# A graph layer with gathered rows: how the edge lists, the statistics and the tables are set up

## The chip, the core and the metric

The kernel runs on one core of a Trainium2 chip. The metric is device time in microseconds (us) of one launch. The core has five engines with instruction streams of their own: PE (TensorE, matrix multiply), DVE (VectorE), ACT (ScalarE), POOL (GpSimd) and SP (SyncE, which here only issues DMA transfers). They meet only at semaphores. Transfers are issued from SP, ACT and POOL; SP's and ACT's go to a hardware queue each (q1 and q10 in the profile), POOL's gathers to a software queue (q0), and all of them share 16 DMA engines.

## The reference

There are N = 6250 nodes with 256 features and E = 100000 edges (src, dst, weight); dst is sorted.

```python
f = _layernorm(x)
h  = segment_sum(w[:, None] * (f @ W1)[src], dst) + b1          # convolution 1
x_ = leaky(concat([h, f[root]]))
x_ = segment_sum(w[:, None] * (x_ @ W2)[src], dst) + b2          # convolution 2
x_ = concat([leaky(x_), h[root]])
x  = x + leaky(x_ @ Wl + bl)
n  = _layernorm(x)
weights = n @ wr + br
sel = top_k(weights, N//2)[:-1]                                  # 3124 nodes
x  = x + n + scatter(sel, weights[sel] * (gelu(n[sel] @ fw1 + fb1) @ fw2 + fb2))
```

## The kernel before

**Nodes.** They are cut into 49 windows of 128 (NW). x lies in xs, one window per 256 columns. The normed rows are made in acc (f_rows is acc from slot A0 = 4 on) and are stored to f_dram, from which the first convolution gathers; the second one gathers from t2_dram ("conv_rows" in the profile). acc later holds the sums of the windows, so it is set to zero between the store and the first sums.

**Edges.** They are padded to 784 tiles of 128 edges (NT). Four tiles are a group, so there are 196 groups (NG); 16 tiles (RING) are a round, and the rounds run from the last to the first. Only 782 tiles hold an edge (781 full ones and 32 edges); the last two are padding with weight 0.

**The gather stream.** POOL issues one indirect DMA for each tile (L276 to L284): 128 rows of 1 KB into a slot of ring, eight groups deep. From the ninth group on it waits on group_used (L280), which DVE raises once the sums of an older group have been taken. For each tile PE multiplies the gathered rows with a 128x128 selection matrix S (L483 to L490) that DVE builds (L768), and DVE adds the group's sums to acc (L776). Where a group crosses into the next window there is a second set, S_more. The second convolution does the same from t2_dram, with the feed-forward part (L579 to L591) between the groups. At the end come a search for the router's threshold and the output.

**The start.** Before the first gather these things happen:
- SP loads x in five chunks XCH of ten windows (the last of nine, L232 to L236); window 48 has only 106 nodes and is a transfer of its own, behind xs_cleared.
- ACT issues the edge loads (L302 to L305): each list goes to a tile of 112 partitions with 7 pieces of 128 edges, as six pieces for all partitions, 109 rows of 128 edges for the seventh and one row for the rest. Then come the same dst values again as rows of 512 (dst_groups, L307 to L311), with 98, 97 and 1 rows.
- POOL turns the lists into floats (L265, L266). PE transposes them into PSUM (L462 to L466). DVE copies them out (L721 to L729) as idx (gather indices), dstc and wc.
- DVE computes the statistics of a chunk (normalise, L693 to L706: bn_stats, bn_aggr, an inverse square root by small steps). ACT applies them (L333 to L337). SP stores the chunk (L237 to L239).
- DVE takes the minimum and maximum of dst per group (L710 to L717), PE spreads them over the partitions (L468 to L473), and DVE makes the tables (L738 to L755).

DVE's order is: memsets, chunks 0 and 1, minimum and maximum, chunk 2, the copies of the turned edges and the root's index, chunks 3 and 4, tables, and, after the stores, memsets of acc (L854 to L857). ACT's order is: all edge loads, a table load for gelu, the five chunks, then the root's row, the weights, and a clear of part of acc (L350). POOL waits for edges_kept (L268) and for all stores (L272) before the first gather.

Of the kernel before, what the change touches and what calls it, by code (L numbers as in the profile page):

```python
# [17 lines left out]
def gnn_ffn_kernel(nc, x, src, dst, edge_weight, W1, b1, W2, b2, Wl, bl, root_idx,  # L18
# [5 lines left out]
    P = 128  # L24
    N, D = x.shape
# [19 lines left out]
    CH = 7  # L45
    CR = NT // CH
    SKEW = 4
# [14 lines left out]
    assert NT == CH * CR and NG == 2 * GR and CR <= P and GR <= P  # L62
# [6 lines left out]
    with ctx:  # L69
# [62 lines left out]
        nmax = sb("gmm", [P, 2, 2], i32)  # L132
# [19 lines left out]
        src_rows = rflat[0:CR, 0:EW].bitcast(i32).rearrange("p (c e) -> p c e", c=CH)  # L152
        dst_rows = rflat[0:CR, EW:2 * EW].bitcast(i32).rearrange("p (c e) -> p c e", c=CH)
        w_rows = rflat[0:CR, 2 * EW:3 * EW].rearrange("p (c e) -> p c e", c=CH)
        bst = rflat[:, 3 * EW:3 * EW + NW * 6].rearrange("p (w s) -> p w s", s=6)

        src_rowsf = rflat[0:CR, 0:EW].rearrange("p (c e) -> p c e", c=CH)
        dst_rowsf = rflat[0:CR, EW:2 * EW].rearrange("p (c e) -> p c e", c=CH)

        f_rows = acc[:, A0:A0 + NW, :]  # L160
        dst_groups = acc[0:GR, A0 + NW:A0 + NW + 2 * GE // D, :].rearrange("p r d -> p (r d)").bitcast(i32).rearrange("p (c e) -> p c e", c=2)
        diag = hT[:, :, :].rearrange("p c n -> p (c n)")[:, 0:4 * GR].rearrange("p (a c g) -> p a c g", a=2, c=2)
# [11 lines left out]
        edges_cleared, edges_loaded = sem("edges_cleared"), sem("edges_loaded")  # L174
        rows_floated, edges_turned, edges_kept = sem("rows_floated"), sem("edges_turned"), sem("edges_kept")
        groups_loaded = sem("groups_loaded")
# [4 lines left out]
        f_ready, f_stored = sem("f_ready"), sem("f_stored")  # L181
# [38 lines left out]
        ZCUT = NACC * 5 // 8  # L220
# [10 lines left out]
        def _(sp):  # L231
# [3 lines left out]
            sp.wait_ge(xs_cleared, 1)  # L235
            sp.dma_start(xs[0:LAST_ROWS, X0 + NW - 1, :], x[(NW - 1) * P:N, :]).then_inc(x_loaded[-1], 16)  # L236
            for c, (w0, w1) in enumerate(XCH):  # L237
                sp.wait_ge(f_ready, c + 1)
                sp.dma_start(f_dram[w0 * P:w1 * P, :].rearrange("(w p) d -> p w d", p=P), f_rows[:, w0:w1, :]).then_inc(f_stored, 16)  # L239
# [9 lines left out]
        def _(pool):  # L249
            link = Links(pool, pool_chain)  # L250

            nc.gpsimd.memset(src_rows[:, CH - 1, :], 0).then_inc(edges_cleared, 1)
            nc.gpsimd.memset(dst_rows[:, CH - 1, :], N - 1).then_inc(edges_cleared, 1)
            nc.gpsimd.memset(w_rows[:, CH - 1, :], 0.0).then_inc(edges_cleared, 1)
            nc.gpsimd.memset(dst_groups[:, 1, :], N - 1).then_inc(edges_cleared, 1)
# [4 lines left out]
            link(nc.gpsimd.memset(ident[:, :], 0.0))  # L260
            nc.gpsimd.affine_select(out=ident[:, :], in_=ident[:, :], compare_op=ALU.not_equal, fill=1.0, base=0,
                                    pattern=[[-1, P]], channel_multiplier=1).then_inc(consts_ready, 1)
# [4 lines left out]
            nc.gpsimd.iota(iota[:, :], pattern=[[1, 2 * P]], base=0, channel_multiplier=0).then_inc(iota_ready, 1)  # L267
# [26 lines left out]
        def _(act):  # L294
# [3 lines left out]
            full = (CH - 1) * CR * P  # L298
            part = (E - full) // P
            rest = E - full - part * P  # L300
            act.wait_ge(edges_cleared, 4)
            for a, r in ((src, src_rows), (dst, dst_rows), (edge_weight, w_rows)):  # L302
# [4 lines left out]
            gfull = E // GE - GR  # L307
            gend = (GR + gfull) * GE
            act.dma_start(dst_groups[:, 0, :], dst[0:GR * GE].rearrange("(r e) -> r e", e=GE)).then_inc(groups_loaded, 16)
            act.dma_start(dst_groups[0:gfull, 1, :], dst[GR * GE:gend].rearrange("(r e) -> r e", e=GE)).then_inc(groups_loaded, 16)  # L310
# [704 lines left out]
```

## Time and profile before

| | us |
|---|---|
| median of 3 runs | 2211.76 |
| lowest and highest run | 2207.11, 2212.53 |
| the profiled execution | 2209.72 |
| its span, first to last instruction | 2207.7 |
| mean granted TensorE clock | 0.915 of full speed |

Busy time in the span: PE 1693.9 us (77%), DVE 1149.4 (52%), ACT 371.0 (17%), POOL 1511.5 (68%). The mean DMA rate is 107 GB/s; in the first two fortieths of the span it is 193 and 183 GB/s. A row of the timeline reads: start, duration, engine, line, operation, output<-inputs, number of instructions merged, and in brackets the idle time of the engine ahead of it with what ended it. SPq and ACTq are the DMA issues of SP and ACT.

### The profile page before, as it was taken

How to read it: one execution, taken by the hardware profiler on the slowest of the kernel's cores; microseconds unless marked ns; L12 is line 12 of the kernel's file. 1: busy time of each engine (PE TensorE's matmuls, PEld its weight loads, DVE VectorE, ACT ScalarE, POOL GpSimd, SP SyncE). 2: the span in 40 equal slices, each digit the busy share in tenths (PEclk: the TensorE clock that was granted, in tenths of full speed). 3: DMA queues.
4: the chain of work that ended last, by engine and by line, in shares of the span. 5: the costliest groups of instructions: out<-in, count | busy, mean ns of one | idle time of the engine just before them, and what ended most of it. 6: DMA issues, size and time to landing. Idle time of an engine off the chain costs nothing.

```text
span 2207.7 us, 39619 instructions
## 1 busy us (share of the span) xinstructions
PE 1693.9 (77%) x7203; PEld 1361.6 (62%) x7204; DVE 1149.4 (52%) x4020; ACT 371.0 (17%) x938; POOL 1511.5 (68%) x1588
## 2 busy tenths in 40 slices
PE   0277777777767766767679999989998999988881
PEld 0165556555545554555468888878777777777660
DVE  5654445444444343333356666666565555555446
ACT  2300000000000000000112222222222222222230
POOL 1377777777777777777577777777777777777500
PEclk9998899888888888887899999999999999999995
DMA  6633333333333333333233333333333333333203
GB/s 193 183 111 109 110 111 109 109 112 111 108 112 112 111 109 110 112 110 109 81 106 104 103 104 102 103 104 105 104 103 104 105 104 103 103 104 105 76 0 116
DMA packets 109339, 236.70 MB, mean 107 GB/s; under 512 B 28862, under 2 KB 58683, under 8 KB 109310
## 3 DMA queue, kind: packets, MB, share of 16 engines
q0 software_dynamic: 75392, 205.62, 31.9%
q1 hardware_dynamic: 19048, 19.22, 2.7%
q10 hardware_dynamic: 14870, 11.58, 1.6%
q14 instruction: 24, 0.20, 0.0%
q8 instruction: 5, 0.08, 0.0%
HBM read 216.94 MB, written 19.38 MB: 107 GB/s over the span
## 4 chain that ended last, share of the span: by engine, by line
POOL 44%; PE 25%; issue 18%; DVE 5%; DMA 4%; DVEq 2%; ACTq 1%; ACT 0%; POOLq 0%
POOL ring L283 44%; PE ps_agg L489 13%; PE ps_dn L583 4%; PE ps_up L590 4%; DMA ring<-conv_rows,idx 2%; DMA ring<-normed_rows,idx 2%; DVE S L768 1%; ACTq L305 1%; DVE xs L990 1%; PE ps_dn L581 1%; PE ps_o L553 1%; PE ps_o L621 1%; DMA acc<-in_dst 1%; DVE acc L776 0%; DVE ring L699 0%
## 5 line engine op out<-in xcount | busy, mean ns | idle before, releaser
L489 PE MATMUL ps_agg<-ring,S 128*128 x3136 | 869.7, 426 | 342.7 <-DMA ring<-normed_rows,idx 162.1
L489 PEld LDWEIGHTS ps_agg<-ring,S 128*128 128x128 f32 x3136 | 643.7, 212 | 511.0 <-issue 416.6
L283 POOL DMA_INDIRECT ring<-normed_rows,idx x784 | 752.0, 959 | 282.8 <-issue 234.1
L283 POOL DMA_INDIRECT ring<-conv_rows,idx x784 | 752.9, 960 | 256.2 <-issue 231.6
L776 DVE TENSOR_TENSOR acc<-acc,ps_agg x490 | 206.5, 421 | 651.3 <-PE ps_agg L489 601.1
L768 DVE TENSOR_SCALAR S<-iota,dstc,wc 128x128 f32<-128x128 int16 x1584 | 448.5, 363 | 153.9 <-issue 124.2
L489 PE MATMUL ps_agg<-ring,S_more 128*128 x768 | 192.2, 395 | 19.8 <-DVE S_more L768 18.1
L583 PE MATMUL ps_dn<-fw2s,hT 128*128 128x256 f32 x864 | 206.2, 393 | 0.0
L590 PE MATMUL ps_up<-xnT,fw1s 128*128 128x256 f32 x832 | 190.5, 382 | 1.2 <-ACT hT L400 1.2
L583 PEld LDWEIGHTS ps_dn<-fw2s,hT 128*128 128x128 f32 x864 | 163.4, 194 | 39.6 <-issue 18.6
L489 PEld LDWEIGHTS ps_agg<-ring,S_more 128*128 128x128 f32 x768 | 150.5, 199 | 54.0 <-issue 32.1
L590 PEld LDWEIGHTS ps_up<-xnT,fw1s 128*128 128x128 f32 x832 | 154.1, 190 | 20.4 <-ACT hT L400 1.6
L364 ACT ACTIVATE stage<-acc 128x256 f32 x103 | 42.9, 417 | 441.5 <-DVEq L802 432.6
L768 DVE TENSOR_SCALAR S_more<-iota,dmore,wc 128x128 f32<-128x128 int16 x384 | 111.0, 365 | 8.9
L400 ACT ACTIVATE hT<-ps_up,fb1c 128x256 f32<-128x256 f32 x212 | 83.0, 478 | 59.7 <-PE ps_up L590 59.7
L374 ACT ACTIVATE xnT<-ps_t 128x256 f32<-128x256 f32 x50 | 19.2, 384 | 436.2 <-PE ps_t L542 426.5
L758 DVE SCALAR_TENSOR_TENSOR zT<-yT 128x256 f32<-128x256 f32 x103 | 44.0, 427 | 40.7 <-DVE acc L776 32.2
L553 PE MATMUL ps_o<-W2s,zT 128*128 128x256 f32 x200 | 59.7, 423 | 0.0
L389 ACT ACTIVATE yT<-ps_h,b1c 128x128 f32<-128x128 f32 x100 | 31.3, 364 | 156.9 <-PE ps_h L562 156.9
L562 PEld LDWEIGHTS ps_h<-xnT,W1s 128*128 128x128 f32 x400 | 55.0, 199 | 3.1
L434 ACT ACTIVATE xn<-rows,norm 128x256 f32<-128x256 f32 x53 | 31.9, 603 | 137.3 <-DVE norm L921 137.3
L562 PE MATMUL ps_h<-xnT,W1s 128*128 128x128 f32 x400 | 54.8, 282 | 0.0
(175 smaller groups left out, 981.9 us busy)
## 6 DMA issues: line engine op xcount, KB each, us to landing
ring<-normed_rows,idx POOLq DMA_INDIRECT x784
ring<-conv_rows,idx POOLq DMA_INDIRECT x784
conv_rows<-rows ACTq DMA_DIRECT2D x50, 128.0 KB
out_rows<-xs SPq DMA_DIRECT2D x6, 896.0 KB
xs<-in_x SPq DMA_DIRECT2D x4, 1280.0 KB, 14.3
normed_rows<-acc SPq DMA_DIRECT2D x4, 1280.0 KB, 5.2
normed_rows<-acc SPq DMA_DIRECT2D x1, 1152.0 KB, 4.8
xs<-in_x SPq DMA_DIRECT2D x1, 1024.0 KB
```

The lines of the kernel that those rows point to most:

```text
L283: pool.indirect_dma_start(out=ring[:, slot * TG + t, :], out_offset=None, in_=f_dram if l == 0 else t2_dram, in_offset=bass.IndirectOffset ...
L364: nc.scalar.activation(stage[:, :], flat(acc[:, ds(within(act.snap(s * -1 + (NW - 1 + A0)), NACC - 1), 1), :]), ACT.Copy).then_inc(staged[ ...
L400: last = nc.scalar.activation(hT[:, b * HB + c, :], ps_up[:, c, :], ACT.Gelu_apprx_tanh, bias=fb1c[:, b * HB + c:b * HB + c + 1])
L434: nc.scalar.activation(xn[:, :], rows[:, :], ACT.Identity, scale=rinv1, bias=nmr1).then_inc(xn_ready, 1)
L489: last = nc.tensor.matmul(to, select[:, t, :], moving, start=(t == 0), stop=(t == TG - 1))
L553: last = nc.tensor.matmul(ps_o[:, 0:D], zT[:, k, :], W2s[:, k, :], start=False, stop=(k == KC - 1))
L562: last = nc.tensor.matmul(ps_h[:, c * P:(c + 1) * P], W1s[:, k, c * P:(c + 1) * P], aggT[:, k, :], start=(k == 0), stop=(k == KC - 1))
L583: last = nc.tensor.matmul(ps_dn[:, 0:D], hT[:, c, window * P:(window + 1) * P], fw2s[:, c, :], start=False, stop=(c == HC - 1))
L590: last = nc.tensor.matmul(ps_up[:, c, :], fw1s[:, k, (b * HB + c) * P:(b * HB + c + 1) * P], xnT[:, k, :], start=(k == 0), stop=(k == KC - 1))
L758: return V.scalar_tensor_tensor(to, of, SLOPE, of, ALU.mult, ALU.max)
L768: last = V.tensor_scalar(to[:, t, :], iota[:, 0:P], at, wc[:, ds(column, 1)], ALU.is_equal, ALU.mult)
L776: V.tensor_tensor(to, to, flat(ps_agg[:, ds((i + 1) & 1, 1), 0:D]), op=ALU.add).then_inc(acc_step[l], 1)
```

## The change

- **Edge lists** are loaded as 98 rows of 1024 edges, 4 KB contiguous per partition: 96 rows in one transfer, one row, and the rest of the last row (672 edges). CH is 8 and CR is 98. The padding is set by three small DVE memsets ahead of all other DVE work, in place of four POOL memsets. The separate dst_groups load is gone: minimum and maximum are taken from the turned-to-float dst rows, two groups a row.
- **Each list has its own semaphore**. POOL clamps src while it turns it to float, then turns dst; PE transposes a list when it is there; **ACT copies** the turned lists out of PSUM (six activations, written with a stride of 8 columns) ahead of its chunk work.
- **DVE** computes the statistics of all five chunks first, then minimum and maximum, the root's index, and the tables.
- **XCH runs from the last node down**: (40, 49), (30, 40), (20, 30), (10, 20), (0, 10). SP waits for xs_cleared and loads window 48 behind the first transfer, ahead of the other four chunks.
- **Clearing acc**: DVE clears slots 0 to 3 at the start; POOL clears each of the first four chunks when it has been stored (2560 columns, the first 2304); ACT clears the last chunk. DVE's two memsets after the stores are gone.
- **Two empty tiles are not gathered**, in each convolution. Their ring slots are cleared by POOL once. PE still multiplies them.
- POOL also waits for diag_ready before the first gather.

```diff
-    CH = 7
+    CH = 2 * TG
+    SPARE = NT - -(-E // P)
@@ sync
-        XCH = [(0, 10), (10, 20), (20, 30), (30, 40), (40, NW)]
+        XCH = [(40, NW), (30, 40), (20, 30), (10, 20), (0, 10)]
...
+                if w1 == NW:
+                    sp.wait_ge(xs_cleared, 1)
+                    sp.dma_start(xs[0:LAST_ROWS, X0 + NW - 1, :], x[(NW - 1) * P:N, :]).then_inc(x_loaded[c], 16)
@@ gpsimd
-            nc.gpsimd.memset(src_rows[:, CH - 1, :], 0).then_inc(edges_cleared, 1)
...
-            pool.wait_ge(edges_loaded, 16 * 9)
-            nc.gpsimd.tensor_copy(src_rowsf[:, :, :], src_rows[:, :, :]).then_inc(rows_floated, 1)
-            nc.gpsimd.tensor_copy(dst_rowsf[:, :, :], dst_rows[:, :, :]).then_inc(rows_floated, 1)
+            nc.gpsimd.memset(spare_rows, 0.0)
+            pool.wait_ge(src_loaded, 16 * 3)
+            nc.gpsimd.tensor_scalar(src_rowsf, src_rows, 0.0, float(N - 1), ALU.max, ALU.min).then_inc(rows_floated, 1)
+            pool.wait_ge(dst_loaded, 16 * 3)
+            nc.gpsimd.tensor_copy(dst_rowsf, dst_rows).then_inc(rows_floated, 1)
...
+            for c, (w0, w1) in enumerate(XCH[:-1]):
+                pool.wait_ge(f_stored[c], 16)
+                nc.gpsimd.memset(acc[:, A0 + w0:A0 + w1, :], 0.0).then_inc(cleared, 1)
             pool.wait_ge(edges_kept, 3)
...
-                    pool.wait_ge(f_stored, 16 * len(XCH))
+                    pool.wait_ge(diag_ready, 1)
+                    pool.wait_ge(f_stored[-1], 16)
...
+                        if tile >= NT - SPARE:
+                            continue
@@ scalar
-                act.dma_start(r[:, 0:CH - 1, :], a[0:full].rearrange("(c r e) -> r c e", r=CR, e=P)).then_inc(edges_loaded, 16)
-                act.dma_start(r[0:part, CH - 1, :], a[full:full + part * P].rearrange("(r e) -> r e", e=P)).then_inc(edges_loaded, 16)
-                act.dma_start(r[part:part + 1, CH - 1, 0:rest], a[full + part * P:E].rearrange("(r e) -> r e", r=1)).then_inc(edges_loaded, 16)
+                act.dma_start(r[0:96, :], a[0:full].rearrange("(r e) -> r e", e=EW)).then_inc(loaded, 16)
+                act.dma_start(r[96:97, :], a[full:more].rearrange("(r e) -> r e", e=EW)).then_inc(loaded, 16)
+                act.dma_start(r[97:98, 0:E - more], a[more:E].rearrange("(r e) -> r e", r=1)).then_inc(loaded, 16)
...
+            for i, (banks, to) in enumerate(zip(turned, columns)):
+                act.wait_ge(edges_turned, i + 1)
+                for h, bank in enumerate(banks):
+                    last = nc.scalar.activation(to.rearrange(by_chunk, c=CH)[:, h * TG:(h + 1) * TG, :], bank[:, 0:TG * CR].rearrange("p (c r) -> p c r", c=TG), ACT.Copy)
+                last.then_inc(edges_kept, 1)
...
+            w0, w1 = XCH[-1]
+            nc.scalar.activation(acc[:, A0 + w0:A0 + w1, :], zeros[:, 0:1].unsqueeze(2).to_broadcast([P, w1 - w0, D]), ACT.Copy).then_inc(cleared, 1)
@@ vector
-            V.memset(acc[:, DUMMY + 1:A0 - 1, :], 0.0)
+            tail = E - (CR - 1) * EW
+            V.memset(src_rows[96:CR, tail:EW], 0)
+            V.memset(dst_rows[96:CR, tail:EW], N - 1)
+            V.memset(w_rows[96:CR, tail:EW], 0.0).then_inc(edges_cleared, 1)
+            V.memset(acc[:, 0:A0, :], 0.0).then_inc(cleared, 1)
...
-            normalise((0, 1))
-
-            dve.wait_ge(groups_loaded, 16 * 3)
+            normalise(range(len(XCH)))
+
+            dve.wait_ge(rows_floated, 2)
...
-            dve.wait_ge(f_stored, 16 * len(XCH))
-            V.memset(acc[:, DUMMY, :], 0.0).then_inc(cleared, 1)
-            V.memset(acc[:, A0 - 1:ZCUT, :], 0.0).then_inc(cleared, 1)
-            dve.wait_ge(cleared, 3)
+            dve.wait_ge(cleared, CLEARS)
```

## Rows read from the trace of the kernel before

**Rows 1.** The page, costliest groups: line, engine, tiles, count | busy, mean ns | idle ahead.

```profile
L283 POOL DMA_INDIRECT ring<-normed_rows,idx x784 | 752.0, 959 | 282.8 <-issue 234.1
```

**Rows 2.** What POOL waited for: us in total, times, the longest one.

```profile
POOL ring L283 <- issue: 465.7, 1528, 0.3
...
POOL ring L283 <- DVEq L798: 11.6, 38, 0.3
```

**Rows 3.** The gathers of L283: shortest/median/longest ns, first and last start in us.

```profile
L283 POOL DMA_INDIRECT ring<-normed_rows,idx x784: 949/953/1168, 81.7 to 1071.4; - x196
L283 POOL DMA_INDIRECT ring<-conv_rows,idx x784: 949/953/1402, 1089.9 to 2080.5; - x196
```

**Rows 4.** Busy time by stage: us, PE, PEld, DVE, ACT, POOL, clock, DMA share, GB/s.

```profile
81.60:1072.40 990.80, 708.28 (x2716) 538.71 (x2716) 432.22 (x1376) 91.19 (x239) 751.99 (x784) 0.87 0.39 114
1072.40:1089.80 17.40, 12.72 (x44) 8.82 (x44) 1.76 (x6) 4.14 (x12) 0.00 (x0) 0.72 0.07 23
1089.80:2081.50 991.70, 903.32 (x4137) 756.91 (x4135) 598.46 (x2189) 227.21 (x575) 752.95 (x784) 0.98 0.35 104
```

**Rows 5.** The chain that ended last, 0 to 200 us: start, duration, what.

```profile
76.00 4.79 DMA normed_rows<-acc
80.83 0.85 issue
```

**Rows 6.** Timeline, 0 to 110 us: the chunks on DVE and on ACT.

```profile
8.78 3.36 DVE L699 BATCH_NORM_STATS2 ring<-xs 128x6 f32<-128x256 f32 x10
...
15.84 3.37 DVE L699 BATCH_NORM_STATS2 ring<-xs 128x6 f32<-128x256 f32 x10
...
43.75 1.22 DVE L711 TENSOR_REDUCE gmm<-acc 98x2 int32<-98x1024 int32 x1 [21.00 <-DMA acc<-in_dst]
...
47.19 3.35 DVE L699 BATCH_NORM_STATS2 ring<-xs 128x6 f32<-128x256 f32 x10
...
54.18 5.02 ACT L336 ACTIVATE acc<-xs,S_more 128x256 f32<-128x256 f32 x10 [7.51 <-DVEq L706]
...
64.82 3.04 DVE L699 BATCH_NORM_STATS2 ring<-xs 128x6 f32<-128x256 f32 x9
...
71.44 4.53 ACT L336 ACTIVATE acc<-xs,S_more 128x256 f32<-128x256 f32 x9 [1.65 <-DVEq L706]
```

**Rows 7.** The same timeline: the last edge load, its cast, the last transposes.

```profile
23.94 6.76 ACTq L305 DMA_DIRECT2D ring<-in_edge_weight  x1
...
35.40 0.93 POOL L265 CAST ring<-ring 112x896 f32<-112x896 int32 x1 [29.35 <-DMA ring<-in_edge_weight]
...
39.99 1.51 PE L465 MATMUL ps_up<-ident,ring 112*128 112x112 f32 x7
```

**Rows 8.** Busy time, 36 to 40 us, while the 97-row piece of dst_groups lands; columns as rows 4.

```profile
36.00:40.00 4.00, 2.65 (x15) 2.68 (x16) 0.00 (x0) 3.99 (x9) 1.50 (x3) 1.00 0.08 25
```

**Rows 9.** The same timeline: memsets of DVE and POOL, and ACT's clear.

```profile
0.98 0.48 DVE L680 MEMSET acc<- 128x512 f32 x1 [0.84 <-PEq L1005]
1.23 0.53 POOL L255 MEMSET acc<- 98x512 int32 x1
...
3.17 0.91 DVE L684 MEMSET ps_agg<- 128x1024 f32 x1 [0.21 <-issue]
...
88.00 4.89 ACT L350 ACTIVATE acc<-vrow 128x5632 f32<-128x5632 f32 x1 [12.03 <-issue]
```

**Rows 10.** DMA queues in 4 to 24 us: packets, MB, share of 16 engines.

```profile
q1 hardware_dynamic: 5656, 5.71, 91.1%
```

**Rows 11.** DMA queues in 92 to 94 us, weights in rows of 4 KB.

```profile
q10 hardware_dynamic: 145, 0.57, 74.8%
```

**Rows 12.** The x chunks of L234, from issue to landing.

```profile
DMA to landing us min/median/max: 6.5/14.3/20.2
```

**Rows 13.** The page, DMA issues: count, KB each, median us to landing.

```profile
normed_rows<-acc SPq DMA_DIRECT2D x4, 1280.0 KB, 5.2
```

**Rows 14.** DVE's copies of L884, beside POOL's gathers: shortest/median/longest ns, starts.

```profile
L884 DVE COPY acc<-vrow x50: 280/294/511, 121.8 to 1083.8; 128x256 f32 x50
```

More of the change, by code:

```diff
@@ L151, in gnn_ffn_kernel @@
         EW = CH * P
-        src_rows = rflat[0:CR, 0:EW].bitcast(i32).rearrange("p (c e) -> p c e", c=CH)
-        dst_rows = rflat[0:CR, EW:2 * EW].bitcast(i32).rearrange("p (c e) -> p c e", c=CH)
-        w_rows = rflat[0:CR, 2 * EW:3 * EW].rearrange("p (c e) -> p c e", c=CH)
+        src_rows, dst_rows = (rflat[0:CR, i * EW:(i + 1) * EW].bitcast(i32) for i in range(2))
+        src_rowsf, dst_rowsf, w_rows = (rflat[0:CR, i * EW:(i + 1) * EW] for i in range(3))
         bst = rflat[:, 3 * EW:3 * EW + NW * 6].rearrange("p (w s) -> p w s", s=6)
-        src_rowsf = rflat[0:CR, 0:EW].rearrange("p (c e) -> p c e", c=CH)
-        dst_rowsf = rflat[0:CR, EW:2 * EW].rearrange("p (c e) -> p c e", c=CH)
+        spare_rows = ring[:, RING - SPARE:RING, :]
+        by_chunk = "p (r c) -> p c r"
         f_rows = acc[:, A0:A0 + NW, :]
-        dst_groups = acc[0:GR, A0 + NW:A0 + NW + 2 * GE // D, :].rearrange("p r d -> p (r d)").bitcast(i32).rearrange("p (c e) -> p c e", c=2)
-        diag = hT[:, :, :].rearrange("p c n -> p (c n)")[:, 0:4 * GR].rearrange("p (a c g) -> p a c g", a=2, c=2)
+        diag = hT[:, :, :].rearrange("p c n -> p (c n)")[:, 0:4 * GR].rearrange("p (a r c) -> p a r c", a=2, c=2)
         ps_agg = pb("ps_agg", [P, 2, 512])
@@ L296, in _ @@
             one = "(o n) -> o n"
[L298 to L302, printed above, removed]
[L303 to L311 removed]
+            full, more = 96 * EW, 97 * EW
+            act.wait_ge(edges_cleared, 1)
+            for a, r, loaded in ((src, src_rows, src_loaded), (dst, dst_rows, dst_loaded), (edge_weight, w_rows, w_loaded)):
+                act.dma_start(r[0:96, :], a[0:full].rearrange("(r e) -> r e", e=EW)).then_inc(loaded, 16)
+                act.dma_start(r[96:97, :], a[full:more].rearrange("(r e) -> r e", e=EW)).then_inc(loaded, 16)
+                act.dma_start(r[97:98, 0:E - more], a[more:E].rearrange("(r e) -> r e", r=1)).then_inc(loaded, 16)
             act.dma_start(rooti[:, 0:1], root_idx[0:1].rearrange(one, o=1).to_broadcast([P, 1])).then_inc(root_loaded, 16)
@@ L331, in _ @@
             nc.scalar.activation(small[:, 7:8], zeros[:, 0:1], ACT.Gelu_apprx_tanh)
+            turned = [(ps_t[:, :], ps_h[:, :]), (ps_o[:, :], ps_dn[:, :]), (up_flat[:, 0:512], up_flat[:, 512:1024])]
+            columns = [idx[:, :], dstc[:, PADT:PADT + NT], wc[:, PADT:PADT + NT]]
+            for i, (banks, to) in enumerate(zip(turned, columns)):
[3 more added lines that the diff above has]
+                last.then_inc(edges_kept, 1)
             for c, (w0, w1) in enumerate(XCH):
@@ L337, in _ @@
                 last.then_inc(f_ready, 1)
-            act.wait_ge(f_stored, 16 * len(XCH))
+            for stored in f_stored:
+                act.wait_ge(stored, 16)
+            w0, w1 = XCH[-1]
+            nc.scalar.activation(acc[:, A0 + w0:A0 + w1, :], zeros[:, 0:1].unsqueeze(2).to_broadcast([P, w1 - w0, D]), ACT.Copy).then_inc(cleared, 1)
             act.wait_ge(root_ready, 1)
@@ L349, in _ @@
             act.wait_ge(tables_ready, 1)
-            nc.scalar.activation(acc[:, ZCUT:NACC, :], zeros[:, 0:1].unsqueeze(2).to_broadcast([P, NACC - ZCUT, D]), ACT.Copy).then_inc(cleared, 1)
             act.wait_ge(weights_loaded, 16 * (N_SMALL + 2))
@@ L471, in _ @@
                 to = (ps_t, ps_o)[i]
-                last = nc.tensor.matmul(to[:, 0:NG], ones[0:GR, :], diag[0:GR, i, :, :].rearrange("p c g -> p (c g)"), start=True, stop=True)
+                last = nc.tensor.matmul(to[:, 0:NG], ones[0:GR, :], diag[0:GR, i, :, :].rearrange("p r c -> p (r c)"), start=True, stop=True)
             last.then_inc(spread_done, 1)
@@ L497, in edge_group @@
                 tile = within(pe.snap((it & 1) * RING + q * TG), SLOTS * TG - TG)
-                pe.wait_ge(landed[0][q], (it >> 1) * LAND + (1 + (NIT + 1) // 2 * l) * LAND)
+                short = 16 * SPARE * (l + 1) if q == QG - 1 else 0
+                pe.wait_ge(landed[0][q], (it >> 1) * LAND + ((1 + (NIT + 1) // 2 * l) * LAND - short))
                 pe.wait_ge(landed[1][q], ((it + 1) >> 1) * LAND + (16 + NIT // 2 * l * LAND))
@@ L735, in _ @@
             dve.sem_inc(root_ready, 1)
-            normalise(range(3, len(XCH)))
+            dve.wait_ge(edges_kept, 3)
             dve.wait_ge(spread_done, 1)
```

56 lines of the change are left out of this document (22 added, 34 removed).

## The prediction

> **What bounds the kernel now.** I began with the costliest groups of the page. POOL's indirect DMAs come to 752 us of busy time in each convolution [rows 1], more than half of the span with both. Then I asked what POOL waited for. All its 1528 + 38 = 1566 idle times between gathers are about 0.30 us (the longest is 0.3), and 1566 is 2 x 783, every gap there is [rows 2]. So POOL never waited for group_used: neither PE nor DVE holds the stream, though the chain of waits steps over to PE now and then. First and last starts give the pitch: (1071.4 - 81.7) / 783 = 1.264 us a gather, and 1.265 in the second convolution [rows 3]. The table by stage says the same: POOL is busy 75.9% of both stretches, which is 0.96 of every 1.26 us, while PE is busy 71% in the first and 91% in the second [rows 4].
>
> So the time is a sum of four pieces: the start up to the first gather (81.7 us), 783 pitches, the turn between the convolutions (17.4 us without a gather [rows 4]), 783 pitches, and a tail of 127 us. The change touches the start, and takes two gathers out of each stream. Everything behind the first gather hangs on it and should move with it as a block.
>
> **The start before**, read backwards. The first gather starts 0.85 us after the last store has landed, which took 4.79 [rows 5]. Ahead of that ACT applied the last chunk (4.53 us from 71.44), and ahead of that DVE computed it from 64.82 [rows 6]. DVE has one long hole: after chunk 1 it waits 21.00 us for the second copy of dst, until 43.75 [rows 6]. And why was that late? The edge loads crawl: the last list is there at 35.40, nearly 12 us after its last piece was issued, and that issue alone held ACT for 6.76 us [rows 7]. At 36 to 40 us, when the 97-row piece of dst_groups is under way, the DMA share is 0.08 of 16 engines, 25 GB/s [rows 8]: that is one engine's worth. A transfer of 97 rows is not spread; neither, I read from the same pattern, is one of 109.
>
> **The change, part by part.**
>
> *DVE's start.* Three memsets of 352 columns come first. From 0.48 us for 512 columns and 0.91 for 1024 [rows 9] 352 columns cost about 0.35: 1.05 in all. Clearing 1024 columns of acc in place of 512 adds 0.43. Statistics could begin at 8.78 + 1.5 = 10.3.
>
> *Chunk 0 of x* is now windows 40 to 48, and window 48 is a transfer of 106 rows, issued when xs_cleared is there (about 4.3 us) and before the other chunks. No row shows how a transfer of 106 rows is spread, so I bound it. A row of 1 KB costs an engine 0.911 x 16 x 20 / 5656 = 0.0515 us [rows 10]. A chunk of 80 rows an engine landed 6.5 us after issue [rows 12], so 2.4 us are fixed. Edges add 18 to 21 rows of 4 KB on the same engine, each 0.748 x 16 x 2 us x 4 KB / 0.57 MB = 0.17 us [rows 11], 3.6 in all. If all 106 rows go to one engine: 0.8 + 2.4 + (64 + 106) x 0.0515 + 3.6 = 15.6. If they are spread over 16: 4.3 + 2.4 + 0.4 = 7.1, before DVE is ready. I take 12.0, nearer the upper end since rows 8 show odd counts on few engines. The Trainium skill, page "DMA: Bandwidth & Descriptors", section "Why a DMA increments its semaphore by 16 and not by 1", says that a transfer gets the largest number up to 16 that divides its rows: two engines for 106, and by that the sum here is 12.8. The same rule speaks for the 96-row loads.
>
> *Five chunks in one go.* A chunk of ten takes 15.84 - 8.78 = 7.06 us on DVE, one of nine 71.44 - 64.82 = 6.62 to ACT's start, one of ten 7.0 to ACT's start (54.18 - 47.19) [rows 6]: 6.67 + 3 x 7.06 + 7.0 = 34.85. ACT starts on the last chunk at 46.85, needs 5.02 [rows 6], the store 5.2 [rows 13], POOL 0.85: first gather at 57.95. The other chunks of x are no limit: 6.4 MB at the rate of before are in by 24 to 30 us, and the last chunk is wanted at 39.9.
>
> *Is ACT free?* It must have started its 49 activations (24.6 us) by about 27. Each list now is 96 rows of 4 KB, 6 an engine, some 1 us, plus two single rows: nine issues of 0.4 to 0.7 us from 2.1 on, the last list landed by 10 to 13. POOL's cast of 896 columns took 0.93 [rows 7], so 1.1 for 1024, up to perhaps 2.5 with the clamp; PE took 1.51 for seven transposes [rows 7], so 1.7 for eight; ACT's six copies of 392 columns some 0.5 each. The copies are over at about 16, and DVE's first statistics come at 18.7. At nothing, with ten microseconds of cover.
>
> *Minimum, maximum, diag* took 43.75 to 47.19, 3.4 us [rows 6]; now they lie behind all statistics, 46.9 to 50.4, and POOL waits for them, but until 57.1 for the store anyway: nothing. The tables (5 us) and the root's index end near 57; PE needs them for the first sums, not POOL for the first 32 tiles.
>
> *Clears.* POOL's memset of 512 columns took 0.53 [rows 9], so 2560 cost 2.7. The fourth lies 7 us ahead of the last store: hidden. ACT's clear of one chunk, 2560/5632 x 4.89 = 2.2 us [rows 9], comes before the root's row and the weights are issued, but DVE's memset of 6.9 and ACT's own 4.89 are gone, so PE starts about as long after the first gather as before. POOL is behind none of it.
>
> *Two gathers less in each stream*: 4 x 1.264 = 5.06 us.
>
> *Sum.* 81.68 - 57.95 = 23.73, and 5.06, makes 28.8. The profiled execution's 2209.7 becomes 2180.9; it lies 2.0 under the median of the runs shown, and on that I add the same: 2183.0. Bounds: statistics from 10.3 give 1.7 less, from 15.6 give 3.6 more; the runs shown spread from -4.7 to +0.8 about their median. The forecast's own range is 2177 to 2188.
>
> **Rivals.**
>
> *A. POOL's clears hold DVE.* Chunk c is stored 10.3 us after its statistics; POOL then writes for 2.7 us. DVE's chunk c+2 comes to its short tensor_scalars 7.06 + 3.4 + 0.8 = 11.3 us after those statistics, right inside. If DVE must wait for POOL's memset, it loses about 1.9 us in each of two or three chunks: 4 to 6 us, 2188. For it: DVE's copies beside POOL's gathers take 280 ns at best and 511 at worst [rows 14]. Against it: DVE's 512 columns took 0.48 while POOL wrote, in line with the 0.91 for 1024 later [rows 9], but that was a memset, not a copy. The Trainium skill, page "SBUF — State Buffer", section "Who interferes with whom", says that copies and tensor_scalars of DVE within SBUF share a port pair with GpSimd and that the later one waits for the whole instruction; by that rule this rival is what happens.
>
> *B. The edges stay slow.* If the last list comes at 35.4 as before [rows 7], the turned copies end near 38.5, and ACT's 24.6 us of activations decide: 38.5 + 24.6 + 5.2 + 0.85 = 69.2 for the first gather. Gain 12.5 + 5.06: 2194. Against: no piece of 97 or 109 rows is left.
>
> *C. Slower: the 96-row transfers go to one engine.* Then 3 x 96 x 0.17 = 49 us of edge rows and 22 of x rows share it, the last list lands near 73, the copies end near 77, the first gather is at 108, 26 later: 2233. This decides the sign from the last list landing later than about 53. Against: 112-partition loads of before ran beside x at 335 GB/s in all [rows 10], which one engine cannot carry.
>
> *D. The gathers taken out bring nothing*, because the stream's lead over PE shrinks and PE becomes the bound in the second convolution, where it is busy 91% [rows 4]: 2188 at most. Against: not one wait for group_used [rows 2].
>
> **How the numbers follow.** Forecast 0.55, A 0.25, B 0.08, C 0.03, D and mixtures of it with others 0.09. The likeliest is the forecast, 2183. The range of 2176 to 2191 takes in the forecast's bounds, A and D, and leaves out B and C. A difference of 0.3% (6.6 us) is about what can be told from none; all cases but C lie at least 17 us below: faster 0.95, within 0.02, slower 0.03.
>
> **What would show it.** The first gather near 58 us, with gaps of 0.30 behind it everywhere; 782 gathers a stream; DVE without a hole but a small one before the first bn_stats, at about 12; edge lists landed by 13 and ACT's copies over by 16; chunk starts on DVE 7.06 apart. A shows as a longer idle time or a longer tensor_scalar in chunks 2 to 4 beside POOL's memsets. B and C show as ACT's chunks back to back, 5.0 apart, behind late copies. The forecast is wrong if the turn or the tail changes length, or if the gather pitch does: 0.01 us of pitch is 16 us of time, more than any term above but the first.

## The result, and the profile of the changed kernel

| | before | after |
|---|---|---|
| median, same job | 2209.6 us | 2174.54 us |
| lowest, highest | 2207.11, 2212.53 | 2173.0, 2176.29 |
| profiled execution, span | 2209.72, 2207.7 | 2176.29, 2174.5 |
| ratio, 95% interval | | 0.9841 (0.9824 to 0.9858) |

The gain is 35.1 us where I had forecast 28.8; the median of 2174.54 lies 1.5 us under the lower end of my range, 2176. Gains and a loss that I had not forecast hide in that difference, and the trace keeps them apart. First the stream, the gathers of the changed kernel (shortest/median/longest ns, first and last start) and what POOL waited for (us in total, times, longest); they answer to [rows 3] and [rows 2].

```profile
L286 POOL DMA_INDIRECT ring<-normed_rows,idx x782: 942/949/1173, 63.6 to 1047.0; - x196
L286 POOL DMA_INDIRECT ring<-conv_rows,idx x782: 942/949/1369, 1063.6 to 2048.9; - x196
```

```profile
POOL ring L286 <- issue: 464.0, 1522, 0.3
...
POOL ring L286 <- DVEq L800: 12.2, 40, 0.3
```

As before, 1522 + 40 = 1562 = 2 x 781 gaps of 0.3 us: the stream is never held up. It starts at 63.6, not at 57.95. But a gather's median is 949 ns in place of 953, and the pitch is 983.4 / 781 = 1.259 us in place of 1.264 in the first convolution, 985.3 / 781 = 1.262 in place of 1.265 in the second. So the spans divide like this:

| piece of the span | before | after | difference | forecast |
|---|---|---|---|---|
| start to first gather | 81.7 | 63.6 | -18.1 | -23.7 |
| first stream | 989.7 | 983.4 | -6.3 | -2.5 |
| turn | 18.5 | 16.6 | -1.9 | 0 |
| second stream | 990.6 | 985.3 | -5.3 | -2.5 |
| tail | 127.2 | 125.6 | -1.6 | 0 |

The start on the timeline (start, duration, engine, line, operation, and the idle time ahead in brackets); it answers to [rows 6].

```profile
8.95 3.64 POOL L258 TENSOR_SCALAR ring<-ring 98x1024 f32<-98x1024 int32 x1 [6.66 <-DMA ring<-in_src]
...
14.93 3.04 DVE L712 BATCH_NORM_STATS2 ring<-xs 128x6 f32<-128x256 f32 x9 [4.42 <-DMA xs<-in_x]
...
17.13 1.63 ACT L333 ACTIVATE wc<-ps_up 128x392 f32<-128x392 f32 x2
...
32.58 2.02 POOL L267 MEMSET acc<- 128x2304 f32 x1 [16.68 <-DMA normed_rows<-acc]
32.87 1.76 DVE L674 TENSOR_SCALAR S_more<-S_more 128x10 f32<-128x10 f32 x1
34.66 0.17 DVE L675 TENSOR_SCALAR S_more<-S_more 128x10 f32<-128x10 f32 x1
...
47.51 2.23 POOL L267 MEMSET acc<- 128x2560 f32 x1 [6.39 <-DMA normed_rows<-acc]
...
48.57 1.20 DVE L674 TENSOR_SCALAR S_more<-S_more 128x10 f32<-128x10 f32 x1
...
52.39 5.02 ACT L339 ACTIVATE acc<-xs,S_more 128x256 f32<-128x256 f32 x10 [3.06 <-DVEq L719]
...
54.58 2.23 POOL L267 MEMSET acc<- 128x2560 f32 x1 [4.83 <-DMA normed_rows<-acc]
54.96 1.88 DVE L727 TENSOR_SCALAR glim<-gmm 98x4 f32<-98x4 f32 x1
```

The order is the forecast one: loads done early, ACT's copies over by 18.8, ACT free. Two things are late. DVE sits idle for 4.42 us until chunk 0 has landed, at 14.93 and not at 12.0. And three tensor_scalars of ten or four columns last 1.76, 1.20 and 1.88 us in place of 0.17; each ends within 0.04 us of the POOL memset beside it (34.63 and 34.60, 49.77 and 49.74, 56.84 and 56.81). The third lies behind the statistics and costs nothing.

One thing has to be said ahead of the experiments: in three of the five jobs (kernels timed together on one chip) that follow, every kernel, the one before too, took a quarter longer (medians of 2748 to 2753 us for the kernel before), with gaps of up to 7 or 10 us in the gather stream (a "held" stream below), so from these jobs I take what happens ahead of the first gather and the duration of a gather, which agree with the other jobs, and compare times only within the job.

### The profile page after: what moved, and what is told of

The parts are those of the page before. It is cut to its first block, busy times and chain, and to the rows that moved or that the text cites. A ratio compares the mean times of both kernels' runs of the same rounds, so it can differ in the third digit from the quotient of the medians.

```text
span 2174.5 us, 39622 instructions
## 1 busy us (share of the span) xinstructions
PE 1687.2 (78%) x7206; PEld 1355.9 (62%) x7207; DVE 1144.2 (53%) x4015; ACT 373.2 (17%) x944; POOL 1512.2 (70%) x1585
## 4 chain that ended last, share of the span: by engine, by line
POOL 41%; PE 29%; issue 17%; DVE 6%; DMA 4%; DVEq 2%; ACT 0%; ACTq 0%
POOL ring L286 41%; PE ps_agg L497 15%; PE ps_dn L592 5%; PE ps_up L599 4%; DMA ring<-conv_rows,idx 1%; DMA ring<-normed_rows,idx 1%; DVE S L770 1%; PE ps_dn L590 1%; DVE xs L989 1%; PE ps_o L562 1%; DVE ring L712 1%; PE ps_o L630 1%; DVE acc L778 1%; PE ps_h L605 1%; PE ps_o L560 0%
## 5 line engine op out<-in xcount | busy, mean ns | idle before, releaser
L770 DVE TENSOR_SCALAR S<-iota,dstc,wc 128x128 f32<-128x128 int16 x1584 | 448.1, 361 | 151.9 <-issue 123.0
L770 DVE TENSOR_SCALAR S_more<-iota,dmore,wc 128x128 f32<-128x128 int16 x384 | 110.8, 364 | 8.9
L630 PE MATMUL ps_o<-Wls,zT 128*128 128x256 f32 x212 | 54.4, 379 | 0.0
```

Source lines behind the costliest of these rows:

```text
L630: last = nc.tensor.matmul(ps_o[:, 0:D], zT[:, k, :], Wls[:, k, :], start=(k == 0), stop=(k == KC - 1))
L770: last = V.tensor_scalar(to[:, t, :], iota[:, 0:P], at, wc[:, ds(column, 1)], ALU.is_equal, ALU.mult)
```

## Experiments

### Is the quicker stream chance, and what are two gathers worth?

**The kernel before again**, unchanged.

> The kernel before, unchanged, with a trace of its own, on the chip that also runs the changed kernel. Theory 1 (the quicker gather stream of the changed kernel belongs to the chip or to chance): the gather's median is 949 ns here too, the pitch 1.259 to 1.262 us, the turn near 16.6 us and the tail near 125.6 us. Theory 2 (it belongs to the changed code): 953 ns and 1.264 to 1.265 us as before, turn 18.5, tail 127. Ratio to the kernel before 1.000 within 0.002 either way; this also shows what the comparison can tell.

Ratio 1.0003 (0.9993 to 1.0012), medians of 2215.3 and 2215.0. Its gathers:

```profile
L283 POOL DMA_INDIRECT ring<-normed_rows,idx x784: 949/953/1123, 81.9 to 1071.3; - x196
L283 POOL DMA_INDIRECT ring<-conv_rows,idx x784: 949/953/1370, 1087.4 to 2078.4; - x196
```

The 953 ns are there again. The turn, though, is 16.1 us here and was 18.5, with the same code: turn and tail wander by some 3 us, and their share in my table is no effect of the change.

**One part alone: two tiles not gathered**, in the kernel before.

```diff
+            nc.gpsimd.memset(ring[:, RING - SPARE:RING, :], 0.0)
...
+                        if tile >= NT - SPARE:
+                            continue
...
```

The rest of the edit makes PE wait for that many landings fewer.

> The kernel before with one part of the change alone: the two empty tiles are not gathered, their ring slots are cleared once. By my sum 4 x 1.264 = 5.1 us less, a ratio of 0.9977, and streams of 782 gathers. Rival D (PE becomes the bound): nothing, ratio 1.000.

Ratio 0.9979 (0.9969 to 0.9988), 2210.03 against 2215.0: 5.0 us, as worked out.

```profile
L287 POOL DMA_INDIRECT ring<-normed_rows,idx x782: 949/957/1366, 81.7 to 1070.2; - x196
```

The median went up to 957 ns, however, in this one profiled execution.

**The changed kernel again**, unchanged.

> The changed kernel again, with a second trace. Theory 1 (chip or chance): its pitch equals that of the kernel before on this chip. Theory 2 (code): 949 ns and 1.259 to 1.262 again whatever the other shows. Ratio 0.984 either way; first gather at 63 to 64 us.

```profile
L286 POOL DMA_INDIRECT ring<-normed_rows,idx x782: 942/946/1179, 63.3 to 1044.7; - x196
L286 POOL DMA_INDIRECT ring<-conv_rows,idx x782: 942/946/1394, 1063.8 to 2045.8; - x196
```

Ratio 0.9832 (0.9816 to 0.9849), 2178.7 against 2215.0. The pitch is 981.4 / 781 = 1.257 us, on the same chip that ran the kernel before with (1071.3 - 81.9) / 783 = 1.264. So it is not the chip. Between these two traces the streams differ by 8.0 and 9.0 us, together 17, of which 5.1 are the gathers left out.

**The change without that part**: all 784 tiles gathered.

```diff
-                        if tile >= NT - SPARE:
-                            continue
...
```

> The changed kernel with all 784 tiles gathered in each convolution. If the two tiles are worth their pitch: 5.1 us above the changed kernel, ratio to before 0.9863. If the quicker pitch comes from leaving gathers out (another place of the instructions, another count in the queue): the gather's median goes back to 953 ns and it is 10 to 12 us above the changed kernel, ratio 0.989.

2183.79 (ratio 0.9859, 0.9843 to 0.9876), 5.1 us above the changed kernel of the job; the gather's median is 949 ns. Leaving gathers out isn't what makes the others quicker.

### What held the start

**97 rows in one transfer**, for each list.

```diff
-                act.dma_start(r[0:96, :], a[0:full].rearrange("(r e) -> r e", e=EW)).then_inc(loaded, 16)
-                act.dma_start(r[96:97, :], a[full:more].rearrange("(r e) -> r e", e=EW)).then_inc(loaded, 16)
+                act.dma_start(r[0:97, :], a[0:more].rearrange("(r e) -> r e", e=EW)).then_inc(loaded, 16)
...
```

> The changed kernel with each edge list loaded as 97 rows of 4 KB in one transfer and one row for the rest. Theory (an odd count of rows stays on one engine, my rival C made real): 97 x 0.17 = 16.5 us of edge rows a list on the engine that also holds its share of x, so src lands near 24 us, dst near 45, the weights near 66; ACT's chunks follow back to back and the first gather is near 100 us, 36 later than in the changed kernel, 2212 in all. If 97 rows are spread over many engines: first gather at 63 to 64 as before, no difference.

Timeline and table by stage of this kernel, and its gathers:

```profile
27.02 3.64 POOL L258 TENSOR_SCALAR ring<-ring 98x1024 f32<-98x1024 int32 x1 [24.73 <-DMA ring<-in_src]
...
47.29 1.04 POOL L260 CAST ring<-ring 98x1024 f32<-98x1024 int32 x1 [16.62 <-DMA ring<-in_dst]
...
70.50 24.13 ACT L338 ACTIVATE acc<-xs,S_more 128x256 f32<-128x256 f32 x49
```

```profile
20.00:30.00 10.00, 0.00 (x0) 0.00 (x0) 6.92 (x32) 0.00 (x0) 2.98 (x1) 1.00 0.07 26
```

```profile
L286 POOL DMA_INDIRECT ring<-normed_rows,idx x782: 940/947/1255, 100.8 to 1324.5; - x196
```

One row more in a transfer makes 37 us. src is there at 27.0 (24 expected), dst at 47.3 (45), and between 20 and 30 us the core moves 26 GB/s at a DMA share of 0.07, one engine in sixteen. ACT's 49 activations follow back to back in 24.1 us and the first gather starts at 100.8, against 100 worked out. The landings came 2 to 3 us later than worked out, the sum within 1. Its one execution took 2776.71 us, beside a median of 2753.32 for the kernel before in this held job; one execution says no more than that it was not quicker. That is the arithmetic of my rivals B and C, confirmed on a case built for it, and it's also why the change splits 98 rows into 96, 1 and 1. The rule behind it, that the number of engines has to divide the number of rows, stands in the Trainium skill, page "DMA: Bandwidth & Descriptors", section "Why a DMA increments its semaphore by 16 and not by 1"; this trace agrees, with its 26 GB/s.

**POOL's clears beside bn_stats**: waits alone are added.

```diff
             for c, (w0, w1) in enumerate(XCH[:-1]):
+                if c + 3 <= len(XCH):
+                    pool.wait_ge(stats_ready, c + 3)
+                else:
+                    pool.wait_ge(diag_ready, 1)
                 pool.wait_ge(f_stored[c], 16)
```

> The changed kernel with POOL's clears moved by waits alone, so that the first three start with a bn_stats or a tensor_reduce of DVE and the fourth behind diag_ready. Theory A (a DVE tensor_scalar waits for a running POOL memset): the 1.76 and 1.20 us of L674 in chunks 2 and 4 go back to 0.17, first gather 2.6 us earlier, at 61.0, ratio 0.9988 to the changed kernel. Rival (those long instructions have another cause): they stay.

The five L674 (here L678) by duration, then the timeline:

```profile
L678 DVE TENSOR_SCALAR S_more<-S_more x5: 171/172/173, 18.3 to 46.5; 128x10 f32<-128x10 f32 x4, 128x9 f32<-128x9 f32 x1
```

```profile
35.22 2.02 POOL L271 MEMSET acc<- 128x2304 f32 x1 [20.12 <-DVEq L723]
35.25 3.37 DVE L716 BATCH_NORM_STATS2 ring<-xs 128x6 f32<-128x256 f32 x10
```

All five are at 0.17 us again, against a longest of 1.76 in the changed kernel, and bn_stats beside the memset takes its usual 3.37. The first gather starts at 60.5, 3.1 us earlier than 63.6 (2.6 expected; chunk 0 also landed 0.5 earlier). Theory A holds. The time says nothing: ratio to before 0.9923 (0.9894 to 0.9952) in a job with a held stream, in which the changed kernel did not run.

**The chunks of x in rising order.**

```diff
-        XCH = [(40, NW), (30, 40), (20, 30), (10, 20), (0, 10)]
+        XCH = [(0, 10), (10, 20), (20, 30), (30, 40), (40, NW)]
```

> The changed kernel with the chunks of x in rising order, so that window 48 is needed last. Theory (the 106-row transfer is what chunk 0 waited for): DVE starts its statistics at 10.5 us in place of 14.9, without a hole, first gather near 57.8, 5 to 6 us earlier. Rival (x itself is late because of the edge rows): DVE still waits for chunk 0, to 13 or later.

```profile
10.55 3.36 DVE L712 BATCH_NORM_STATS2 ring<-xs 128x6 f32<-128x256 f32 x10
...
36.04 2.23 POOL L267 MEMSET acc<- 128x2560 f32 x1 [1.15 <-DMA normed_rows<-acc]
36.06 2.25 DVE L674 TENSOR_SCALAR S_more<-S_more 128x10 f32<-128x10 f32 x1
...
57.87 1.06 POOL L286 DMA_INDIRECT ring<-normed_rows,idx  x1 [4.44 <-DMA normed_rows<-acc]
```

DVE starts at 10.55 without a wait (I had worked out 10.3 for its memsets), and the first gather is at 57.9, 5.7 us earlier. So window 48 made chunk 0 late, and the edge rows alone did not. On how many engines its 106 rows lie can be read here, because window 48 is now the last of x. The table by stage, shortly before the next store:

```profile
30.30:30.60 0.30, 0.00 (x0) 0.00 (x0) 0.26 (x2) 0.00 (x0) 0.00 (x0) 0.50 0.13 48
```

A DMA share of 0.13 with 48 GB/s is two engines of sixteen still at work on rows of 1 KB (of window 48 or of the first store, queued behind it) while the other fourteen are done. That fits two engines for the 106 rows; the profile does not say which rows an engine moves. The collision with POOL's memset is still there, in one chunk now, for 2.1 us. Ratio 0.9907 (0.9878 to 0.9937), beside 0.9923 and 0.9914 of its neighbours: no difference can be read.

**Both.**

> Both: rising chunks and POOL's clears beside bn_stats. If the two add: first gather near 55.5 us, 8 us under the changed kernel, ratio to the kernel before 0.980. The gather's median in all three is a further sample of its spread: in 942 to 950 if it belongs to the changed code, up to 957 if it is chance.

First gather at 55.7, so the two add; the gather's median is 947, 946 and 946 ns in the three. Ratio 0.9914 (0.9885 to 0.9943), not the 0.980 expected. In a second job with a held stream:

> The kernel with rising chunks and POOL's clears beside bn_stats again, on another chip: where the gather stream is not held up, the 7.9 us that its first gather gained over the changed kernel (55.7 against 63.6) must come out whole. Expected: 8 us under the changed kernel, ratio to the kernel before 0.980, 2170 us.

55.6, ratio 0.9891 (0.986 to 0.9922). In a third, beside the changed kernel:

> The changed kernel unchanged, so that the others of this job have it beside them on the same chip at the same time. Median of the gather 946 to 949 ns, first gather 63 to 64 us, ratio to the kernel before 0.984 where the stream is not held up, 0.990 where PE and DVE hold it (gaps of several us between gathers).

> Rising chunks and POOL's clears beside bn_stats, beside the changed kernel of this job: first gather at 55.7, 8 us earlier than in the changed kernel, and 8 us in the whole (ratio to before 0.980) where the stream is not held up; where it is held up, a part of the 8 may be lost in the waits.

First gathers at 63.6 and 55.8; 0.9923 (0.9898 to 0.9947) against 0.9894 (0.9858 to 0.993), medians of 2724.62 and 2716.24. The intervals overlap, so the 8 us are not shown here. What held the stream there shows in POOL's waits, first of the changed kernel in this job, then of the changed kernel in a job with an undisturbed stream:

```profile
POOL ring L286 <- DVEq L800: 536.4, 186, 7.0
POOL ring L286 <- issue: 421.2, 1370, 1.0
```

```profile
POOL ring L286 <- issue: 463.0, 1520, 0.3
...
POOL ring L286 <- DVEq L800: 12.8, 42, 0.3
```

186 groups of four tiles, of the 376 that could (188 in each convolution, the ring being free for the first eight), now wait for group_used, up to 7 us; in the undisturbed job the 42 gaps that the profile puts down to DVE take the 0.3 us of any gap. So in these jobs the consumers bound the kernel for long stretches, and what is saved in POOL's stream is partly lost in them: the change brings 0.8% there, 24 us (2748.31 less 2724.62), in place of 35. It is not the chip alone: the chip of the first experiments, where the stream ran free, also ran the second of the held jobs.

The pair once more:

> The changed kernel unchanged, beside the next kernel. If the stream is not held up in this job: ratio 0.984, first gather 63 to 64 us. If it is (gaps of several us between gathers): 0.992.

> Rising chunks and POOL's clears beside bn_stats. First gather at 55.7. If the stream is not held up: 8 us under the changed kernel of this job, ratio 0.980. If it is: 2 to 8 us under it, as in the two jobs before (0.989 against 0.992).

This time the stream ran free. The changed kernel: 2175.12 (2174.57 to 2177.8), ratio 0.9846 (0.9833 to 0.986). Both edits: **2169.78** (2169.22 to 2170.64), ratio 0.9818 (0.9805 to 0.9832), against 2210.26 for the kernel before. That is 5.3 us better than the changed kernel (8 expected, and a ratio of 0.980, which lies just outside the interval), with a first gather at

```profile
L290 POOL DMA_INDIRECT ring<-normed_rows,idx x782: 942/946/1208, 55.7 to 1037.8; - x196
```

in place of 63.1. Of the 7.4 us in the start 2.0 went in the turn between the profiled executions (18.4 against 16.4, no work of this edit), which is within what that stretch wanders.

### The two halves of the change

**Statistics first, alone**, in the kernel before (old loads).

```diff
-            normalise((0, 1))
+            normalise(range(len(XCH)))
...
-            normalise((2,))
-            normalise(range(3, len(XCH)))
```

> The kernel before with one part alone: all statistics first, minimum and maximum, copies of the turned edges and tables behind them. The old edge loads stay, so ACT is held by its issues until 35.4 and then needs 24.6 us for its 49 activations, or more if DVE's copies hold it. Expected: first gather at 67.5, 14 us earlier than before, ratio 0.9935. Rival (without the new loads nothing is gained, because ACT and the copies come late): first gather above 78, ratio 0.999.

```profile
36.80 24.17 ACT L336 ACTIVATE acc<-xs,S_more 128x256 f32<-128x256 f32 x49
```

```profile
L283 POOL DMA_INDIRECT ring<-normed_rows,idx x784: 947/953/1271, 66.7 to 1300.0; - x196
```

DVE has all statistics by 45, but ACT, held by its issues until 35.4, works them off without a break: first gather at 66.7, 15.0 us earlier. Ratio 0.9934 (0.991 to 0.9957).

**New loads with DVE's old order**, in the changed kernel.

```diff
-            normalise(range(len(XCH)))
+            normalise((0, 1))
...
+            normalise((2,))
...
+                dve.wait_ge(edges_turned, i + 1)
+                for h, bank in enumerate(banks):
+                    last = V.tensor_copy(to.rearrange(by_chunk, c=CH)[:, h * TG:(h + 1) * TG, :], bank[:, 0:TG * CR].rearrange("p (c r) -> p c r", c=TG))
...
+            normalise((3, 4))
```

> The changed kernel with DVE's old order: chunks 0 and 1, minimum and maximum, chunk 2, DVE's own copies of the turned edges, the root, chunks 3 and 4. The new loads stay. Expected: 3.5 us for minimum and maximum, 3.4 for the copies, 0.6 for the root on the path, first gather at 69 to 71, 6 to 8 us above the changed kernel. If the new loads were worth nothing alone: 80 or more.

```profile
28.77 1.22 DVE L717 TENSOR_REDUCE gmm<-ring 98x2 f32<-98x1024 f32 x1 [0.15 <-DVE S_more L710]
```

First gather at 69.4, 12.3 us earlier than before; ratio 0.9964 (0.994 to 0.9987). The 21.00 us that DVE waited ahead of this reduce [rows 6] are gone, because dst is there in time; with the statistics first they are gone because DVE has the chunks to do meanwhile. So each half alone brings 12 to 15 us of the start and both together 18.1: they remove the same wait from two sides. This second half is not the loads alone: the changed kernel's order of chunks and its clears are in it too.

### Why is a gather shorter?

**POOL's loads of fb2 behind its first memsets and its iota**, in the kernel before, near where the changed kernel has them.

```diff
-            pool.wait_ge(xs_cleared, 1)
-            for q in range(QG):
-                part = slice(q * D // QG, (q + 1) * D // QG)
-                pool.dma_start(fb2r[:, part], fb2[part].rearrange("(o n) -> o n", o=1)).then_inc(landed[1][q], 16)
...
             nc.gpsimd.iota(iota[:, :], pattern=[[1, 2 * P]], base=0, channel_multiplier=0).then_inc(iota_ready, 1)
+            pool.wait_ge(xs_cleared, 1)
+            for q in range(QG):
+                part = slice(q * D // QG, (q + 1) * D // QG)
+                pool.dma_start(fb2r[:, part], fb2[part].rearrange("(o n) -> o n", o=1)).then_inc(landed[1][q], 16)
             pool.wait_ge(edges_kept, 3)
```

> The kernel before with POOL's four small loads of fb2 moved behind its casts and iota, as the changed kernel has them; a look at the gather's duration only. If the order of POOL's work ahead of the stream makes the quicker gather: median 946 to 950 ns and a pitch under 1.262. If not: 953 to 957 and 1.264 or more. First gather at 81 to 82 either way.

```profile
L283 POOL DMA_INDIRECT ring<-normed_rows,idx x784: 940/946/1266, 82.3 to 1318.7; - x196
```

946 ns in this one execution of a held stream: it looked as if the place of these loads made it. The pitch can't be read where the stream is held. The same four loads put back at the head of POOL's work, in the changed kernel:

```diff
+            pool.wait_ge(xs_cleared, 1)
+            for q in range(QG):
+                part = slice(q * D // QG, (q + 1) * D // QG)
+                pool.dma_start(fb2r[:, part], fb2[part].rearrange("(o n) -> o n", o=1)).then_inc(landed[1][q], 16)
             link(nc.gpsimd.memset(ident[:, :], 0.0))
...
```

> The changed kernel with one part undone: POOL's four small loads of fb2 stand ahead of its first memset and its casts again, as in the kernel before. Theory (their place sets the duration of every later gather): median 953 ns in place of 946 to 949, pitch 0.004 to 0.007 us longer, 6 to 11 us above the changed kernel where nothing else holds the stream. Rival (chance, or another part of the change): median 942 to 949 as in all traces of the changed code, no difference in time. First gather at 63 to 64 us either way.

```profile
L286 POOL DMA_INDIRECT ring<-normed_rows,idx x782: 943/949/1381, 63.4 to 1271.3; - x196
```

949 ns, within what the changed kernel shows anyway, and no 953. The time, in a held job: 2730.41 us against 2724.62 for the changed kernel, ratios 0.9938 (0.991 to 0.9966) and 0.9923 (0.9898 to 0.9947), no difference that can be read. The move in the kernel before, timed:

> The kernel before with those four loads behind POOL's casts and iota, now timed. Theory: the gather's median is 946 ns again, and the kernel is 6 to 11 us under the kernel before (ratio 0.995 to 0.997), with its first gather at 82 us as before. Rival: no difference in time, ratio 1.000; the 946 of the first look was chance.

949 ns, ratio 1.0028 (0.9995 to 1.006) with a held stream: the theory's 0.995 to 0.997 lies outside. The move goes with a shorter gather in both traces of the kernel before that have it, but undoing it doesn't give a longer one in the changed kernel. The theory that the place of these loads by itself sets the duration falls; whether it is one of several causes no run shows.

## Why the prediction was right and wrong

- **What bounds the kernel**: right. No gap in the stream above 0.3 us in either kernel, so what the start gains goes straight into the time. The crawl of a transfer of 97 rows and ACT's 24.6 us gave the first gather to within a microsecond where they were put to the test (100.8 against 100, 66.7 against 67.5).
- **Two gathers less**: right, 5.0 and 5.1 us measured, 5.06 forecast. Rival D falls wherever the stream runs free.
- **Chunk 0 at 12.0**: mis-sized, 14.93. The larger part is the price of an edge row. I took 0.17 us for 4 KB from a stretch in which weights were loaded [rows 11]. The DMA queues of the changed kernel between 6 and 10 us (packets, MB, share of 16 engines):

```profile
q10 hardware_dynamic: 274, 0.94, 97.1%
q1 hardware_dynamic: 54, 0.06, 5.8%
```

  0.971 x 16 x 4 / 0.94 MB is 0.27 us for 4 KB, and x hardly moves meanwhile (0.06 MB). With 0.27 for 21 rows in place of 0.17 and two engines for 106 rows (my 12.8), the sum gives 12.8 + 2.1 = 14.9. I had taken 12.0 between two bounds, 0.8 under the sum for two engines; both errors had one sign. Cost: 2.9 us. This sum was made after the result; what the runs show by themselves is the late landing and, with the chunks in rising order, that window 48 is its cause.
- **Rival A**, which I gave 0.25 and left out of the sum, is what happened: 1.6 + 1.0 us in two chunks (4 to 6 expected, from memsets of 2.7 us each; they took 2.02 and 2.23). The trace of before could not show it, because no tensor_scalar of DVE within SBUF ran beside a POOL memset there. The Trainium skill, page "SBUF — State Buffer", section "Who interferes with whom", did say it, and also that DVE's instructions with at most one SBUF input outside the two-port modes do not wait. The runs agree on the tensor_scalars: 1.76 and 1.20 us beside the memset, 0.17 without. bn_stats took 3.37 either way. 57.95 + 2.9 + 2.6 is 63.5; measured 63.6.
- **POOL's clamp** took 3.64 us, over my upper end of 2.5, and ACT's six copies some 0.7 us each from start to start in place of 0.5; they were over at 18.8, not at 16. Both lie under the cover that I had named, and cost nothing. Two slips of the working change nothing either: the sum for the first gather is 57.92 as its terms stand, and the 335 GB/s are of both hardware queues together, while the row in [rows 10] is one of them (5.71 MB in 20 us).
- **The gather's pitch, which I put at nothing: the step that failed.** I wrote that 0.01 us of pitch is 16 us, and then assumed none, without a reason. It fell by 0.0048 and 0.0035 us in the first pair of traces, 6.5 us over both streams, and by 0.0070 and 0.0083 in the second, 12.0 us. The start brought 5.6 and 5.1 us less than forecast. With both, 28.8 becomes 29.7 in the first pair and 35.7 in the second.
- **Turn and tail**, the other terms that I put at nothing, gave 3.5 us more in the first pair and took 4.5 in the second (19.1 and 128.7 against 16.1 and 127.2). No edit touches them, and they move by this much between executions of one kernel. With them the spans come out, 33.2 and 31.1 us apart.
- **From the spans to the medians.** The medians differ by 35.1 and 36.3 us, because a profiled execution is not the median one: in the second pair the kernel before was profiled at 2207.54, 7.8 us under its median, and the changed one 2.5 under its own. And the forecast of 2183.0 hung on a median of three runs, 2211.76, where four gave 2209.6. So the 8.5 us between 2183.0 and 2174.54 are 6.5 of pitch, 3.5 of turn and tail, 2.2 of the median that I began from and 1.9 of the place of the profiled executions, less the 5.6 that the start fell short. That the start's two losses don't show in the total is luck, and the range, missed by 1.5 us, would have held without any one of the four gains. That some 12 us are there beyond the start and the gathers left out is not luck of one execution: the medians of the three undisturbed jobs leave 11.9, 12.6 and 11.5 us.
- **Cause of the pitch: open.** The gather's median was 953, 953, 953 and 957 ns in four traces with the old order of POOL's first work, 946 and 949 in two traces of the kernel before with the fb2 loads moved, and 946 to 949 in all fourteen traces of the changed kernel and its variants. It moves by some 3 ns between executions of one and the same kernel (949, 946, 946 and 946 for the changed one), and the old order's 953 to 957 does not overlap with its 946 to 949. So part of it is drawn anew and part goes with the program; leaving gathers out and the place of four small loads alone don't explain it, and DVE's old order in the changed kernel keeps 949, all statistics first in the kernel before keeps 953. Which part of the change does it was not found.

## What to carry to other kernels

When one engine issues a stream of 1500 short instructions and never waits, ask two things: what holds its first one, and what its pitch may do; a step of 4 ns is 6 us here and no edit's cost shows it. So give the pitch a range of its own in the sum, not a zero. Split the rows of a transfer into 96 and a remainder rather than 97, and put an awkward remainder last in its queue or where nobody waits for it: 97 rows in place of 96 + 1 cost 37 us, window 48 ahead of its neighbours 4.4. Work that is moved to POOL for free is free only beside the right DVE instructions: put it beside bn_stats or a reduce.

## What the runs showed of the hardware

- A DVE tensor_scalar within SBUF, four or ten columns wide, waits for a running POOL memset to its end (1.76, 1.20, 1.88, 2.25 us in place of 0.17, each end within 0.04 us of the memset's). Not all of DVE does. Beside such a memset bn_stats takes 3.37 us as ever, a reduce 1.22 (POOL's clears beside bn_stats), a tensor_scalar of one column 0.15 (the same run), and in the changed kernel with DVE's old order copies out of PSUM take 0.87, as behind it, and small operations on two SBUF tensors 0.17:

```profile
49.48 2.23 POOL L267 MEMSET acc<- 128x2560 f32 x1 [8.25 <-DMA normed_rows<-acc]
49.53 0.17 DVE L676 SCALAR_TENSOR_TENSOR S_more<-S_more 128x10 f32<-128x10 f32 x1
49.74 0.17 DVE L674 TENSOR_TENSOR S_more<-S_more 128x10 f32<-128x10 f32 x1
```

- Three transfers of 96 rows of 4 KB with their remainders, issued from ACT, took 97.1% of the 16 DMA engines between 6 and 10 us, and the queue with 1 KB rows 5.8%, though it had rows waiting: SP had issued the next chunk at 4.98.
- The changed kernel took 2173 to 2180 us in some jobs and 2709 to 2731 in another, and the kernel before 2207 to 2221 and 2732 to 2766. The changed kernel's first gather (63.1 to 63.6 us) and the duration of its gathers (946 to 949 ns) were the same in both. The extra time is in DVE's and PE's streams: POOL waits for DVE 182 to 193 times in such a trace and is busy almost as long as ever (1516.0 us in place of 1509.0), while DVE's idle time ahead of L770 with nothing to wait for was 414.1 us in place of 122.9, and its longest 8.7 in place of 1.3. In the held job DVE also waits 96 times, 372.8 us in all, for something that the profile only calls remote, and PE's 7206 matmuls are busy for 1819.2 us in place of 1694.6 at a mean granted clock of 0.845 in place of 0.913. On PE some 125 us of the 534 between the two spans are thus in the matmuls and the rest in idle time; whether the lower clock brings the waits or the waits the lower clock no run tells. Below, the changed kernel in the two kinds of job: DVE's idle time ahead of its selections (in total, times, longest).

```profile
DVE S L770 <- issue: 414.1, 439, 8.7
```

```profile
DVE S L770 <- issue: 122.9, 184, 1.3
```
